# Attention and expert kernel on one core: moving SP's transfers at the change of phase, and one group's row statistics on VectorE

## The chip, the cores and the metric

One Trainium2 chip (trn2), one core. The metric is the device time of one execution in microseconds (us). Of a kernel several executions are timed and the median is given.

## The reference

The input x is (8, 512, 128) in float32: 8 batches of 512 tokens. It is layer-normed, and the result goes two ways: through causal attention with 16 heads of 8 (relu on queries, keys and values, a mask for keys and queries whose row sums to zero, a residual and a layer norm), and through a second norm, a product, eight experts and a last product with gelu. The two are multiplied, with silu on the second, and added to x.

```
xn = layernorm(x)                                # eps 1e-5
Q, K, V = relu(xn @ Wq + bq), relu(xn @ Wk + bk), relu(xn @ Wv + bv)
scores = Q K^T / sqrt(8), causal, masked where a row of xn sums to 0
s = gamma * norm(softmax(scores) V + xn) + beta
f = norm2(xn) @ attn_w.T + attn_b + xn
h = gelu(f_e @ w1[e] + b1[e]);  eo = h @ w2[e] + b2[e]      # expert e takes 256 tokens of each half
g = silu(gelu(eo @ next_w.T + next_b))
out = x + s * g
```

## The kernel before

The program is written engine by engine, with semaphores, in two blocks that meet at a barrier.

**The first phase** (L261 to L793) works batch by batch, i = 0 to 7. VectorE (DVE) norms x: `means` and `variances` per group of tiles (GROUPS, L32: batches 0 to 3, 4 and 5, 6 and 7), then per batch `quotients(i)` (L511) and `sums(i)` (L529), a reduction for the second norm. GpSimd (POOL) refines square roots (`first_roots`, `second_roots`, L346 to L386) and adds up the sums (`totals(i)`, L394). ScalarE (ACT) makes the second norm (`second_norm`, L599, which waits for `totals`) and moves results out of PSUM. TensorE (PE) transposes (`second_normed`, L706, waits for `second_norm`), then projects and runs the experts. Queries and keys go to DRAM as three bf16 parts each: ACT's `split` writes the first (L641, L642), DVE's `rests(i)` (L542) takes the remainder, ACT's `mids` the second, DVE's `lows(i)` (L548) the third. SP stores them (`store_parts`, L251): 4 transfers for queries (one is of constant rows), 5 for keys. On DVE the order in the loop of L569 is quotients(i), sums(i), lows(i-2), rests(i-1). `statistics` (L555) of the last group, `means`, `variances` and `seeds` in one piece, stands at i = 4 behind rests(3), and POOL's `first_roots` of that group waits for its seeds. `hold` (L736) issues products whose result nobody reads; LATE_ROWS (L53) puts 6 before `second_normed(2)` and 8 before `second_normed(5)`.

**The second phase** (L860 on) works in 32 units: batch b, group g of four heads. Keys and queries are stacked on 124 partitions of four tiles: an even batch lies in `q_own`/`k_own`, an odd one in the rooms of the expert weights, `w1_room`/`w2_room` (w_room in the trace). A stack holds the parts (72 rows), a mask row, three rows with the scores' maxima, ones against these (`ones_b`), and 48 fixed rows (`bar_k`, `bar_q`) that carry the causal mask. PE's `chunk` (L1192) makes scores two units ahead for DVE's maxima (L1037, 11 a unit), POOL splits these, PE transposes them (L1210), ACT copies them (`mT`, L1133), and SP writes them as a row into the query stack (L866). PE's unit u starts with a wait for that row (`mrow_in`, L1257), then goes on with the products `keys` (L1213), for ACT's exponentials (L1156), and `values` (L1228).

**SP's queue at the change of phase** is what the change is about. SP waits for the last `lows`, then stores batch 7's parts (9 transfers), issues `load_fixed(sp, 1)` (L174: the fixed rows of the odd stacks, three transfers of 48, 768 and 768 KB), and only then the row for unit 0, `maxima(tok, 0, 0)`. Behind it come per unit the next row and the loads for the unit four further on (7 transfers, `load`). PE meanwhile makes the scores of units 0 and 1 with a product of no use behind each (L1310), to the end of the warm-up.

```
903  sp.wait_ge(low_ready, B)
904  for o in range(2):
905      store_parts(sp, B - 1, o)
906  sp.wait_ge(w2_done, B)
907  load_fixed(sp, 1)
908  maxima(tok, 0, 0)
```

## Time and profile before

| | |
|---|---|
| median of 3 executions | 452.3 us (452.23 to 453.25) |
| the profiled execution | 450.58 us |
| its span in the profile | 448.7 us |
| first phase / second phase, by the trace | 0 to 163.8 us / 163.8 to 448.7 us |
| PE / DVE / ACT / POOL busy | 84% / 82% / 64% / 45% of the span |
| mean granted clock of TensorE | 0.966 of full speed |

Durations and instants in this text are those of the profiled execution; instants count from the start of its span. A row of a timeline gives start, busy time, engine, line, operation, output and inputs, the number of instructions merged into it, and in brackets the idle time before it with what ended it. "SPq" is SP's queue while it issues a transfer; the time on the transfer's way to its place is shown as "DMA" in the chain.

### The profile page before, as it was taken

Reading aid. Unit: us, or ns where it says so; the run is one execution under the profiler, and the core shown is the slowest. Engines: PE = TensorE matmul, PEld = TensorE weight load, DVE = VectorE, ACT = ScalarE, POOL = GpSimd, SP = SyncE. Lnnn points to the kernel's source line nnn. Section 1 sums busy time; section 2 is a strip of 40 time slices with the busy share of each in tenths; the row PEclk is TensorE's granted clock in tenths of the full one; section 3 lists DMA queues with packets and bytes.
Section 4 is the critical chain, followed back from the end, with each engine's and each line's share of the span. In section 5 each row is a group of like instructions: output and inputs, shape, how many; then the busy total and the mean of one; then the engine's idle time right before and its main releaser. Section 6 shows DMA issues by size and latency. Waiting matters only on the chain.

```text
span 448.7 us, 9664 instructions
## 1 busy us (share of the span) xinstructions
PE 375.1 (84%) x3507; PEld 246.3 (55%) x3507; DVE 366.9 (82%) x846; ACT 288.7 (64%) x572; POOL 201.4 (45%) x525
## 2 busy tenths in 40 slices
PE   0046997999799985499999999999999999999950
PEld 0013774787487752366656665566566566656420
DVE  5989998979794257379899898999998998989427
ACT  0004777887588921367877877868778778778740
POOL 8422284417531131002147456556374474565591
PEclk9999999999899999599999999999999999999985
DMA  8920003772545527233332424342422424240000
GB/s 218 329 69 1 1 12 99 172 163 54 154 121 139 139 68 155 37 90 80 89 81 72 121 59 114 82 104 65 125 68 76 119 72 122 59 112 27 3 23 23
DMA packets 32197, 41.71 MB, mean 93 GB/s; under 512 B 5926, under 2 KB 24726, under 8 KB 32150
## 3 DMA queue, kind: packets, MB, share of 16 engines
q1 hardware_dynamic: 31990, 41.08, 34.8%
q8 instruction: 27, 0.44, 0.4%
q14 instruction: 20, 0.16, 0.1%
q0 software_dynamic: 160, 0.03, 0.0%
HBM read 26.43 MB, written 11.02 MB: 83 GB/s over the span
## 4 chain that ended last, share of the span: by engine, by line
PE 43%; DVE 12%; DMA 3%; SPq 2%; issue 2%; ACT 1%; POOL 0%; DVEq 0%; ACTq 0%; POOLq 0%
PE banks L1238 15%; PE banks L1221 8%; PE banks L1201 8%; DVE mx L1037 7%; PE banks L1203 5%; PE banks L1223 5%; DMA q_own<-mT 3%; DVE res L1076 2%; DVE stats L1082 2%; PE banks L1248 1%; SPq L256 1%; ACT pt L1156 1%; SPq L179 1%; PE banks L1210 0%; DVE res L1063 0%
## 5 line engine op out<-in xcount | busy, mean ns | idle before, releaser
L1037 DVE TENSOR_REDUCE mx<-banks 128x1 f32<-128x512 f32 (+3 forms) x352 | 200.9, 635 | 28.3 <-PE banks L1203 26.4
L1156 ACT ACTIVATE pt<-banks 128x512 f32<-128x512 f32 x320 | 169.8, 601 | 56.4 <-PE banks L1223 48.7
L1238 PE MATMUL banks<-pt,vg 128*18 128x512 f32 (+3 forms) x1024 | 81.4, 435 | 0.7 <-ACT pt L1156 0.7
L928 POOL TENSOR_SCALAR mneg<-mx 128x16 f32<-128x16 f32 x32 | 8.1, 253 | 120.7 <-DVE mx L1037 119.5
L1201 PE MATMUL banks<-k_own,q_own 76*128 76x384 bf16 (+2 forms) x192 | 49.9, 283 | 13.2 <-DMA q_own<-mT 10.1
L1201 PE MATMUL banks<-w_room 76*128 76x384 bf16 (+2 forms) x192 | 48.1, 274 | 3.4 <-DVE mx L1037 3.4
L1221 PE MATMUL banks<-q_own,k_own 76*128 76x384 bf16 (+2 forms) x192 | 49.4, 283 | 0.0
L1221 PE MATMUL banks<-w_room 76*128 76x384 bf16 (+2 forms) x192 | 47.5, 275 | 0.9 <-ACT pt L1156 0.5
L1238 PEld LDWEIGHTS banks<-pt,vg 128*18 128x18 f32 x1024 | 23.7, 97 | 43.8 <-issue 33.4
L1203 PE MATMUL banks<-k_own,q_own 124*128 124x128 bf16 x256 | 45.1, 224 | 0.0
L1203 PE MATMUL banks<-w_room 124*128 124x128 bf16 x256 | 43.8, 219 | 0.0
L1223 PE MATMUL banks<-q_own,k_own 124*128 124x128 bf16 x256 | 43.6, 224 | 0.0
L1223 PE MATMUL banks<-w_room 124*128 124x128 bf16 x256 | 42.2, 219 | 0.0
L739 PE MATMUL banks<-bias_rows,ones_p 128*128 128x512 bf16 x44 | 12.3, 437 | 28.1 <-DVEq L502 28.1
L1201 PEld LDWEIGHTS banks<-k_own,q_own 76*128 76x128 bf16 x192 | 19.0, 100 | 24.4 <-DMA q_own<-mT 10.4
L777 PE MATMUL banks<-xaT,w_room 128*128 128x256 f32 x128 | 29.2, 381 | 0.8 <-ACT xaT L620 0.8
L785 PE MATMUL banks<-hid,w_room 128*128 128x256 f32 x128 | 28.9, 379 | 0.0
L677 ACT ACTIVATE hid<-banks,cols_sb 128x256 f32<-128x256 f32 x64 | 26.8, 470 | 1.5 <-PE banks L777 0.9
L1221 PEld LDWEIGHTS banks<-w_room 76*128 76x128 bf16 x192 | 18.7, 97 | 14.8 <-ACT pt L1156 6.3
L1223 PEld LDWEIGHTS banks<-q_own,k_own 124*128 124x128 bf16 x256 | 25.9, 101 | 1.1
L1221 PEld LDWEIGHTS banks<-q_own,k_own 76*128 76x128 bf16 x192 | 19.3, 101 | 13.0 <-issue 4.1
L777 PEld LDWEIGHTS banks<-xaT,w_room 128*128 128x128 f32 x128 | 23.7, 190 | 4.6 <-ACT xaT L620 1.6
(196 smaller groups left out, 732.6 us busy)
## 6 DMA issues: line engine op xcount, KB each, us to landing
k_scratch<-parts SPq DMA_DIRECT2D x40, 128.0 KB, 2.3
k_own<-k_scratch SPq DMA_DIRECT2D x48, 96.0 KB
w_room<-k_scratch SPq DMA_DIRECT2D x48, 96.0 KB
q_scratch<-parts SPq DMA_DIRECT2D x24, 128.0 KB, 2.3
q_own<-q_scratch SPq DMA_DIRECT2D x32, 96.0 KB
w_room<-q_scratch SPq DMA_DIRECT2D x32, 96.0 KB
w_room<-in_w_dram SPq DMA_DIRECT2D x1, 2048.0 KB, 11.9
q_own<-q_scratch SPq DMA_DIRECT2D x16, 112.0 KB
```

The lines of the kernel that those rows point to most:

```text
L677: ins = act.activation(hid[:, h, j, :], banks[:, bank + j // 2, EC * (j % 2):EC * (j % 2) + EC], ACT.Gelu, bias=b1[2 * n + h][j])
L739: mm(banks[:, TRX, :], ones_p[:, :], bias_rows[:, 0:1, :].broadcast_to([P, TB, C]), start=True, stop=True)
L777: ins = mm(banks[:, bank + j // 2, EC * (j % 2):EC * (j % 2) + EC], w1_sb[:, 2 * n + h, P * j:P * j + P], xaT[:, EC * h:EC * h + EC], star ...
L785: ins = mm(banks[:, XB, EC * h:EC * h + EC], w2_sb[:, 2 * n + h, j, :], hid[:, h, j, :], start=(j == 0), stop=(j == HC - 1))
L1037: dve.tensor_reduce(mx[:, u % 2, heads[0]:heads[-1] + 1, q], banks[:, S0 + slots[0] % SLOTS, 0:w * len(heads)].rearrange("p (h k) -> p h k ...
L1076: ins = dve.scalar_tensor_tensor(out=res[:, k, :], in0=att[:, k, :], scalar=live_all[:, at:at + 1], in1=xn_all[:, at, :], op0=ALU.mult, op ...
L1156: act.activation(pt[:, T * j:T * j + T], banks[:, bank(), :], ACT.Exp, scale=SCALE).then_inc(exp_done, 1)
L1201: mm(o[:, 0:w - P], qx[by][0:LIVE, g, h, P * q:P * q + P], kx[by][0:LIVE, g, h, 0:w - P], start=True, stop=True)
L1203: ins = mm(o[:, w - P:w], qx[by][0:STACK, g, h, P * q:P * q + P], kx[by][0:STACK, g, h, w - P:w], start=True, stop=True)
L1221: mm(o[:, P:n], kx[par][0:LIVE, g, h, P * k:P * k + P], qx[par][0:LIVE, g, h, P * k + P:T], start=True, stop=True)
L1223: ins = mm(o[:, 0:P], kx[par][0:STACK, g, h, P * k:P * k + P], qx[par][0:STACK, g, h, P * k:P * k + P], start=True, stop=True)
L1238: ins = mm(banks[32 * h:32 * h + VP, OT, P * k:T], vg[:, g, k, h, :], pt[:, KPLACE[k, h]:KPLACE[k, h] + n], start=(k == 0 and g % 2 == 0), ...
```

## The change

Three edits.

1. The fixed rows are loaded in four pieces, one for each group of heads, each with its own semaphore (three transfers of 12, 192 and 192 KB). For the even stacks the four pieces follow each other where the one load stood. For the odd stacks piece g goes behind the row for unit g + 1, ahead of the loads for the odd batch's group g. PE waits for a piece where it first needs it.
2. Of batch 7's stores the query ones stay ahead of the first row; the five key ones go behind the loads of batch 1's units (two, one, one, one).
3. On DVE the last group's `means` and the centring move to i = 3, its `variances` and `seeds` to i = 4, both ahead of `rests`. The 8 idle products before `second_normed(5)` go.

```diff
-LATE_ROWS = {2: 6, 5: 8}
+LATE_ROWS = {2: 6}
...
-    def load_fixed(sp, par):
-        sp.dma_start(kx[par][MROW + 1:LIVE].rearrange("p g h t -> p (g h) t"),
-                     ones_b[:, :].unsqueeze(1).broadcast_to([PARTS, HEADS, T])).then_inc(fixed_in[par], 16)
+    def load_fixed(sp, par, g):
+        sp.dma_start(kx[par][MROW + 1:LIVE, g],
+                     ones_b[:, :].unsqueeze(1).broadcast_to([PARTS, G, T])).then_inc(fixed_in[par][g], 16)
         for stack, bar in ((kx[par], bar_k), (qx[par], bar_q)):
-            sp.dma_start(stack[LIVE:STACK].rearrange("p g h t -> p (g h) t"),
-                         bar[:, :].unsqueeze(1).broadcast_to([BAR_ROWS, HEADS, T])).then_inc(fixed_in[par], 16)
+            sp.dma_start(stack[LIVE:STACK, g],
+                         bar[:, :].unsqueeze(1).broadcast_to([BAR_ROWS, G, T])).then_inc(fixed_in[par][g], 16)
...
+        def store_keys(sp, i, copies):
+            for k in copies:
+                dst = k_dram[i:i + 1, k].rearrange("b d h t -> (b h) d t")
+                sp.dma_start(dst, parts[:, i % 2, 1, k % PARTS, :]).then_inc(parts_out[i % 2][1], 16)
...
                     if i == 1:
                         sp.wait_ge(bars_ready, 1)
-                        load_fixed(sp, 0)
+                        for g in range(NG):
+                            load_fixed(sp, 0, g)
...
+                    if i == 3:
+                        means(GROUPS[2])
+                        centred(GROUPS[2])
+                    if i == 4:
+                        variances(GROUPS[2])
+                        seeds(GROUPS[2])
                     if i > 0:
                         rests(tok, i - 1)
                     if i == 1:
                         dve.wait_ge(x_in[2], 16)
                         statistics(GROUPS[1])
-                    if i == 4:
-                        statistics(GROUPS[2])
...
                         if not last:
+                            if b == 0:
+                                load_fixed(sp, 1, g)
                             load(b + 1, 1 - par, g)
+                            if b == 1:
+                                store_keys(sp, B - 1, range(g, 2 * PARTS - 1, NG))
...
                 sp.wait_ge(low_ready, B)
-                for o in range(2):
-                    store_parts(sp, B - 1, o)
                 sp.wait_ge(w2_done, B)
-                load_fixed(sp, 1)
+                store_queries(sp, B - 1)
                 maxima(tok, 0, 0)
...
                         if ahead:
-                            if first and g == 2:
-                                pe.wait_ge(fixed_in[1], 48)
+                            if u + 2 < 2 * NG:
+                                pe.wait_ge(fixed_in[(u + 2) // NG][(u + 2) % NG], 48)
```

`store_parts` is split into `store_queries` and `store_keys`, and the first line of `variances`, which subtracts the mean, becomes `centred`; the other calls keep their order.

SP's queue from the barrier on, before. `parts` are batch 7's parts, `mT` the row of maxima, here for units 0 and 1 (two rows in one):

```order
L256 DMA q_scratch<-parts 16x8x512 [waits low_ready]
L256 DMA q_scratch<-parts 16x8x512 x2
L258 DMA q_scratch<-q_fixed 16x4x512
L256 DMA k_scratch<-parts 16x8x512 x5
L176 DMA w_room<-ones_b 3x16x512 [waits w2_done]
L179 DMA w_room<-bar_k 48x16x512
L179 DMA w_room<-bar_q 48x16x512
L866 DMA q_own<-mT 3x16x128 [waits mT_ready] x2
L159 DMA w_room<-q_scratch 24x2048 x2
```

The same place now:

```order
L255 DMA q_scratch<-parts 16x8x512 [waits w2_done,low_ready]
L255 DMA q_scratch<-parts 16x8x512 x2
L256 DMA q_scratch<-q_fixed 16x4x512
L882 DMA q_own<-mT 3x16x128 [waits mT_ready] x2
L176 DMA w_room<-ones_b 3x4x512
L179 DMA w_room<-bar_k 48x4x512
L179 DMA w_room<-bar_q 48x4x512
L159 DMA w_room<-q_scratch 24x2048 x2
```

The five key stores and the fixed rows no longer stand ahead of the first two rows of maxima; a quarter of the fixed rows stands behind the second.

DVE behind sums(4), before: `parts<-rest` is lows(2), `rest<-full` is rests(3), and the statistics of the last group follow, seeds at their end:

```order
L551 TENSOR_TENSOR parts<-rest,parts 128x2x512 [waits mid_ready]
L545 TENSOR_TENSOR rest<-full,parts 128x1024 [waits split_ready,low_ready]
L94 TENSOR_REDUCE s<-x_all 128x128 [waits rest_ready]
L96 TENSOR_TENSOR s<-s 128x64 [waits dve_self]
L97 TENSOR_TENSOR s<-s 128x32 [waits dve_self]
L99 TENSOR_TENSOR s<-s 128x16 [waits dve_self]
L100 TENSOR_TENSOR small<-s 128x8 [waits dve_self]
L451 TENSOR_SCALAR small<-small 128x8 [waits dve_self]
L458 TENSOR_TENSOR xn_all<-x_all,small 128x1024 [waits dve_self]
L459 TENSOR_TENSOR gate_all<-xn_all 128x1024 [waits dve_self]
```

The same place now (rows of the first part stand one batch earlier, between lows(1) and rests(2)):

```order
L560 TENSOR_TENSOR parts<-rest,parts 128x2x512 [waits mid_ready]
L468 TENSOR_TENSOR gate_all<-xn_all 128x1024 [waits low_ready]
L469 TENSOR_REDUCE win<-gate_all 128x32 [waits dve_self]
L471 TENSOR_TENSOR small<-win 128x8 [waits dve_self]
L472 TENSOR_TENSOR small<-small,win 128x8 [waits dve_self]
L473 TENSOR_TENSOR small<-small,win 128x8 [waits dve_self]
L474 TENSOR_SCALAR small<-small 128x8 [waits dve_self]
L475 TENSOR_SCALAR small<-small 128x8 [waits dve_self]
L481 TENSOR_SCALAR small<-small 128x2x8 [waits dve_self]
L482 TENSOR_SCALAR small<-small 128x2x8 [waits dve_self]
L554 TENSOR_TENSOR rest<-full,parts 128x1024 [waits dve_self,split_ready]
L524 TENSOR_TENSOR quo<-xn_all,small 128x512 [waits rest_ready]
```

rests(3) now stands behind the seeds, and quotients(5) right behind rests(3).

## Rows read from the trace of the kernel before

**Rows 1.** Chain of waits in order of time, 163 to 190 us (start us, us, what).
```profile
173.77 11.34 DMA q_own<-mT
```

**Rows 2.** Timeline of SP's queue, the key stores (start us, us, engine line op out<-in).
```profile
166.33 3.93 SPq L256 DMA_DIRECT2D k_scratch<-parts  x5
```

**Rows 3.** Timeline of ACT, second norm of batch 4 and the first row's copy.
```profile
95.71 1.64 ACT L602 ACTIVATE xl_st<-xn_all,shift,small 128x128 f32<-128x128 f32 x4
...
172.50 0.27 ACT L1133 ACTIVATE mT<-banks 48x128 bf16<-48x128 bf16 x1 [10.00 <-PE banks L1210]
```

**Rows 4.** Timeline of PE at the hand-over and at two units' starts.
```profile
174.67 0.38 PE L1310 MATMUL banks<-k_own,q_own 76*128 76x512 bf16 x1
185.16 0.50 PE L1201 MATMUL banks<-k_own,q_own 76*128 76x384 bf16 x1 [10.11 <-DMA q_own<-mT]
...
194.87 0.33 PE L1201 MATMUL banks<-k_own,q_own 76*128 76x384 bf16 x1
...
202.09 0.33 PE L1201 MATMUL banks<-w_room 76*128 76x384 bf16 x1
```

**Rows 5.** Busy time by stretch: us, PE, PEld, DVE, ACT, POOL, granted clock, DMA share, GB/s.
```profile
66.00:71.00 5.00, 2.42 (x12) 1.23 (x10) 4.79 (x13) 1.61 (x5) 3.89 (x10) 1.00 0.62 168
...
116.50:121.00 4.50, 4.50 (x20) 3.43 (x21) 4.31 (x12) 3.40 (x6) 3.46 (x12) 0.64 0.69 202
...
185.00:190.00 5.00, 4.84 (x28) 3.37 (x29) 3.26 (x6) 2.90 (x6) 0.00 (x0) 0.50 0.00 0
```

**Rows 6.** Timeline of PE in the first phase.
```profile
98.23 0.60 PE L709 MATMUL banks<-ident,xl_st 128*128 128x128 f32 x4
...
111.90 1.89 PE L739 MATMUL banks<-bias_rows,ones_p 128*128 128x512 bf16 x8
116.43 0.66 PE L709 MATMUL banks<-ident,xl_st 128*128 128x128 f32 x4 [2.64 <-ACT xl_st L602]
...
131.98 0.66 PE L709 MATMUL banks<-ident,xl_st 128*128 128x128 f32 x4 [0.23 <-ACT xl_st L602]
```

**Rows 7.** Timeline of POOL in the first phase.
```profile
91.55 0.20 POOL L405 TENSOR_TENSOR shift<-shift,small 128x4 f32<-128x4 f32 x1
...
111.96 1.23 POOL L399 TENSOR_TENSOR s<-s 128x32 f32<-128x32 f32 x1
...
114.44 0.20 POOL L405 TENSOR_TENSOR shift<-shift,small 128x4 f32<-128x4 f32 x1
...
125.59 1.10 POOL L399 TENSOR_TENSOR s<-s 128x32 f32<-128x32 f32 x1 [4.72 <-DVE s L532]
126.76 1.15 POOL L400 TENSOR_TENSOR s<-s 128x16 f32<-128x16 f32 x1
```

**Rows 8.** Timeline of DVE in the first phase.
```profile
78.43 1.23 DVE L545 TENSOR_TENSOR rest<-full,parts 128x1024 f32<-128x1024 f32 x1 [1.71 <-ACT parts L642]
...
92.08 1.23 DVE L545 TENSOR_TENSOR rest<-full,parts 128x1024 f32<-128x1024 f32 x1 [1.90 <-ACT parts L642]
...
101.72 0.74 DVE L515 TENSOR_TENSOR quo<-xn_all,small 128x512 f32<-128x512 f32 x1
```

**Rows 9.** Timeline of POOL, the mask's store and its reload.
```profile
153.78 0.77 POOL L424 DMA_DIRECT2D mask_scratch<-maskT  x1 [14.31 <-ACT maskT L670]
156.41 2.03 POOL L171 DMA_DIRECT2D k_own<-mask_scratch  x4 [1.86 <-DMA mask_scratch<-maskT]
```

**Rows 10.** Timeline of DVE, row maxima of two warm-up units and of one unit.
```profile
164.45 12.18 DVE L1037 TENSOR_REDUCE mx<-banks 128x1 f32<-128x512 f32 x22 [4.12 <-PE banks L1203]
...
195.07 6.23 DVE L1037 TENSOR_REDUCE mx<-banks 128x4 f32<-128x512 f32 x11 [1.63 <-PE banks L1203]
```

**Rows 11.** Timeline of the SP queue, one unit's row and loads.
```profile
190.34 1.27 SPq L159 DMA_DIRECT2D w_room<-q_scratch  x3
...
192.88 0.65 SPq L171 DMA_DIRECT2D w_room<-mask_scratch  x1
198.55 0.74 SPq L866 DMA_DIRECT2D q_own<-mT  x1
```

More of the change, by code:

```diff
@@ L150, in build_program @@
     mask_in = sem("first_mask_in")
-    fixed_in = [sem("fixed_in_even"), sem("fixed_in_odd")]
+    fixed_in = [[sem(f"fixed_in{par}_{g}") for g in range(NG)] for par in range(2)]
     banks = ctx.enter_context(nc.psum_tensor("banks", [P, 8, 512], F32))
@@ L249, in build_program, with store_queries @@
         mean, var, a, v2, y, y2, t, t2, s, sh, sl, r, nr, rem, t3 = (small[:, k, :] for k in range(15))
-        def store_parts(sp, i, o):
-            for k in range((PARTS, 2 * PARTS - 1)[o]):
-                part = k_dram[i:i + 1, k] if o == 1 else q_dram[i:i + 1, DH * k:DH * k + DH]
-                dst = part.rearrange("b d h t -> (b h) d t")
-                sp.dma_start(dst, parts[:, i % 2, o, k % PARTS, :]).then_inc(parts_out[i % 2][o], 16)
-            if o == 0:
-                sp.dma_start(q_dram[i, PARTS * DH:QROWS].rearrange("r h t -> h r t"),
-                             q_fixed[:, :, :]).then_inc(parts_out[i % 2][0], 16)
+        def store_queries(sp, i):
+            for k in range(PARTS):
+                dst = q_dram[i:i + 1, DH * k:DH * k + DH].rearrange("b d h t -> (b h) d t")
+                sp.dma_start(dst, parts[:, i % 2, 0, k, :]).then_inc(parts_out[i % 2][0], 16)
+            sp.dma_start(q_dram[i, PARTS * DH:QROWS].rearrange("r h t -> h r t"),
+                         q_fixed[:, :, :]).then_inc(parts_out[i % 2][0], 16)
+        def store_keys(sp, i, copies):
+            for k in copies:
+                dst = k_dram[i:i + 1, k].rearrange("b d h t -> (b h) d t")
+                sp.dma_start(dst, parts[:, i % 2, 1, k % PARTS, :]).then_inc(parts_out[i % 2][1], 16)
         with nc.Block() as block:
@@ L278, in _ @@
                     sp.wait_ge(low_ready, tok.next(low_ready))
-                    for o in range(2):
-                        store_parts(sp, i, o)
+                    store_queries(sp, i)
+                    store_keys(sp, i, range(2 * PARTS - 1))
                     if i == 1:
                         sp.wait_ge(bars_ready, 1)
-                        load_fixed(sp, 0)
+                        for g in range(NG):
+                            load_fixed(sp, 0, g)
                     if 2 <= i < 2 + NG:
@@ L451, in means, with centred @@
                     link(dve.tensor_scalar(mean[:, at], mean[:, at], 1.0 / C, None, ALU.mult))
-                def variances(group):
+                def centred(group):
                     t0, n = group
@@ L458, in variances @@
                     link(tt(cen[:, at, :], xg, mean[:, at].unsqueeze(2).broadcast_to([P, n, C]), ALU.subtract))
+                def variances(group):
+                    at = slice(group[0], group[0] + group[1])
                     link(tt(work[:, at, :], cen[:, at, :], cen[:, at, :], ALU.mult))
@@ L557, in statistics @@
                     means(group)
+                    centred(group)
                     variances(group)
@@ L563, in _ @@
                 means(LOADS[0])
+                centred(LOADS[0])
                 variances(LOADS[0])
@@ L566, in _ @@
                 means(LOADS[1])
+                centred(LOADS[1])
                 variances(LOADS[1])
@@ L903, in _ @@
                 sp.wait_ge(low_ready, B)
-                for o in range(2):
-                    store_parts(sp, B - 1, o)
                 sp.wait_ge(w2_done, B)
-                load_fixed(sp, 1)
+                store_queries(sp, B - 1)
                 maxima(tok, 0, 0)
@@ L1302, in batch @@
                         outputs(tok)
-                pe.wait_ge(fixed_in[0], 48)
                 tok = Tokens(pe)
                 for u in range(2):
+                    pe.wait_ge(fixed_in[0][u], 48)
                     pe.wait_ge(stack_in[0][u], tok.next(stack_in[0][u], UNIT_DMAS))
```

## The prediction

> **What bounds the kernel now.** I read the chain of waits first, in order of time, since the shares of busy time (PE 84%, DVE 82%) tell only that both phases are well filled. Through the second phase the chain lies on PE, unit after unit, and nothing in the change touches a unit from batch 2 on. The place to see is the hand-over between the phases at 163.8 us: the chain runs through SP's queue there, and then, from 173.77 us, 11.34 us through one transfer, the row of maxima for unit 0 [rows 1]. Ahead of that 12 KB row stand five key stores, whose issue alone takes 3.93 us [rows 2], and the fixed rows of the odd stacks, 1.6 MB. The row's data was ready at 172.77 us [rows 3]. PE ends its warm-up at 175.05 us (174.67 + 0.38), then waits 10.11 us for the row and starts unit 0 at 185.16 us [rows 4]. The stretches by clock then show what follows the wait: the granted clock is 0.50 from 185 to 190 us, that is 1.2 GHz, the lower level of the two [rows 5]. Unit 0 takes 9.71 us (194.87 - 185.16), unit 1, mostly at full clock, 7.22 us (202.09 - 194.87) [rows 4].
>
> The second place is in the first phase, which I read by the timelines of PE, DVE and POOL. PE runs without a gap up to 111.90 us, issues the 8 idle products, and then waits 2.64 us, to 116.43 us, for ACT's second norm of batch 5 [rows 6]. ACT waited for POOL's totals(5), at work from 111.96 to 114.64 us [rows 7]. POOL was late because it first had to refine the last group's roots, and their seeds come from the statistics that DVE finished just before quotients(5) at 101.72 us [rows 8]. After it the clock falls too: its mean is 0.64 from 116.5 to 121 us [rows 5].
>
> **The hand-over, step by step.** With key stores and fixed rows gone from in front, SP issues four query stores, is done at about 166.3 us, where the first key store is issued now [rows 2], and waits for the row's data. The row is issued at 172.8 us. Before never shows such a row on an empty queue; the nearest case is the mask's small store, 2.63 us from its issue at 153.78 us to the reload that waits for it at 156.41 us [rows 9]. Bounds: 1.9 us (the idle part of that wait) and 3.9 us (the issue time of the five key stores, as an upper mark for a busy queue). I take 2.6: row there at about 175.5 us, PE idle for 0.4 us. That is 9.7 us sooner than 185.16.
>
> Unit 0 then runs at full clock, since PE's break is 0.4 us instead of 10.1. Three things bound the start of unit 1. PE's own work is at most the 7.22 us of unit 1: 182.7. The second row is issued 3.68 us after a unit's start (198.55 - 194.87) and needs 2.6: 181.8. DVE's 22 warm-up maxima end at 176.63 us and the next 11 take 6.23 us [rows 10]: 182.9, less up to a few maxima that PE may be ahead. I take 182.3, against 194.87: **12.6 us** won at the hand-over, with 11.0 (a slower row and DVE's backlog) and 13.0 as its ends. In other terms 9.7 of these are the wait and 2.9 the clock.
>
> Where the stall goes, the next thing late could be the moved transfers. The fixed rows of a quarter go behind the second row, about 180.0 us. Price of a piece: the whole lot, with the row behind it and what was left of the key stores, took 14.9 us (170.26 to 185.11 [rows 1, 2]), so a quarter is 3.7 us at most if it scales; at the other end only three issues count, at the 0.6 us between a load's 0.46 (3.2 over seven) and a key store's 0.79: 1.9 us. Then come seven loads, issued from 190.34 to 193.53 us before, 3.2 us [rows 11]. So SP is free at 185.1 to 186.9 us, and the row for unit 2 is due at 182.3 + 3.7 = 186.0 and needed at 189.5. Cover is there but thin, about 1 us behind the row's own 2.6. I take 0 and keep 1 us a unit for four units as the far end. PE's six waits for the pieces stand where it waits for the loads issued behind them: 0. The key stores, 5 times 0.8 us of issue [rows 2], fall in batch 1 behind the loads, where SP idles about 5 us a unit (193.53 to 198.55 [rows 11]), and they are read only with batch 7: 0.
>
> **The first phase, step by step.** DVE does the same work in another order. Before, it idles 1.71 us ahead of rests(2) and 1.90 us ahead of rests(3), both times for ACT [rows 8]; now one half of the statistics stands ahead of each. The whole is 8.4 us long (93.31, the end of rests(3), to 101.72), a half about 4, so both gaps are filled: quotients(5) starts 3.6 us sooner, at 98.1 us. quotients(4) starts some 2.5 us later instead. Its totals were ready at 91.75 us [rows 7], and ACT took them up at 95.71 [rows 3]: of the 4.0 us of slack 2.5 go to that, and up to 1.2 to the meeting of totals(4) with DVE's next products. It is thin, but holds: 0, with 0.5 us as the far end. Since rests(3), 1.23 us, now stands behind the seeds instead of ahead, these come 4.9 us sooner, and with them POOL's root refinement and totals(5), at about 107.1 us.
>
> There totals(5) meets lows(3) and rests(4) on DVE. Before, its instructions took 1.23 us and then 0.2 each; totals(6), under the same two DVE operations, took 1.10 and 1.15 for its first two [rows 7]. That is 0.9 us more, so totals(5) ends at 110.7 instead of 114.64, **4.0 us** sooner. The Trainium skill (SBUF, State Buffer, section SBUF: two separate sides) says that DVE with two SBUF inputs and a reading GpSimd operation exclude each other for a whole instruction; by that rule, the trace agrees, it is 4.0, and without it the sum would have 4.9.
>
> PE's second_normed(5) then starts at 112.4 instead of 116.43, and DVE's next batch, which waits for POOL's halves behind the totals, 4.0 us sooner too. From there on all goes the same way: totals(6) is again slow, and second_normed(6) comes at 128.0 instead of 131.98 [rows 6]. PE, at full clock now, would be there at about 126.1 (112.4 and a period of 13.7 us, as from 98.23 to 111.90 [rows 6]), so it idles 1.9 us. The lower clock behind 116.43 therefore gives nothing back, since DVE and POOL, not PE, set 131.98. The idle products gone are 1.89 us of PE that were hidden by the wait; left in, they would end at 113.8 and cost 1.4. The nine more transfers of the even stacks' pieces add some 6 us of issue behind the stores of batch 1; these are 9 issues of 0.7 us in a period of 13.7, and the first loads come a batch later, so 7 us were free: 0.
>
> **Sum.** 12.6 + 4.0 = 16.6 us. Against the profiled execution, 450.58 us, that gives 434.0. The median of the runs shown is 452.3, 1.7 above; the same step gives **435.7 us**.
>
> **Rivals.**
> 1. The clock falls in the first phase, after the new 1.9 us wait at 126 us. Against: between 66 and 71 us PE was busy for 2.42 of 5 us and the clock stayed at 1.00; for: the wait before 116.43 us did bring it down [rows 5]. Price: 15.55 us between 116.43 and 131.98 against 13.7 at full clock, up to 1.9 us: 437.6 us.
> 2. The pieces are slow and delay rows 2 to 5. For: the same transfers held the row for 11.34 us [rows 1]. Against: each is a quarter. At 1 us a unit, four units: 439.7 us. The Trainium skill (DMA: Bandwidth & Descriptors, Bandwidth) speaks against cutting transfers: "Transfers under 64 KB are descriptor-dominated", and its advice is 1 MiB. By that rule the 12 KB pieces and 192 KB pieces cost more than a quarter each, which would lead here; the trace has no piece of this kind.
> 3. The row's wait is not the queue but the row's own way. Then only the issue moves, 173.77 to 172.8, 1 us: 447.3 us. Against: the other 31 rows are never waited for.
> 4. Slower: each piece holds the queue so long that rows 2 to 5 each come late by more than 4.2 us (a quarter of 16.6). That needs a piece of over 8 us, where I have at most 3.7: loads 3.2, piece 8, against a pitch of 7.2. At 14 us a piece, that is, if a piece costs what the whole does, each unit takes 17 us instead of 7.2: 435.7 + 39 = 475 us.
> 5. The change doesn't do what it says: the row is held by the query stores still ahead. Their issue is over at 166.3, 6.5 us ahead of the row's; this goes with rival 3.
>
> **Numbers.** Forecast 0.66, rival 1 0.15, rival 2 0.12, rivals 3 and 5 0.04, rival 4 0.02, and 0.01 for no change at all. A measurement of this kernel can tell about 0.3%, 1.4 us, from no change. Range: low, the hand-over at 13.0, POOL undisturbed (4.9), and a median as low as the profiled run (1.7 less): 432.7, rounded to 432.5. High, rival 2 with 0.8 us to spare: 440.5. Faster 0.97, same 0.01, slower 0.02.
>
> **What would show it.** PE's wait for `mT` under 1 us, the granted clock at 1.0 over the hand-over, unit 0 under 7.5 us; SP's pieces behind the second row, no PE wait for `mT` or the rooms in units 2 to 7; quotients(5) 3.6 us sooner, PE's wait before second_normed(5) under 1 us and before second_normed(6) about 1.9. Wrong would be: new waits for the row in batch 0, a clock under 1 at 128 us, or a barrier that moves by less than 3 us.

## The result and the profile after

The changed kernel takes 434.19 us in the median (433.81 to 434.34, 4 executions) against 452.26 us (451.46 to 453.25, 4): ratio 0.9598, 95% interval 0.9578 to 0.9618. Forecast were 435.7 us, in a range from 432.5 to 440.5. The medians are 18.1 us apart, the two profiled executions only 16.8 us (450.58 and 433.81 us; spans 448.7 and 432.1). In a second comparison, below, the medians were 434.16 and 451.04 us, 16.9 apart; before's own executions spread over more than 2 us, and what goes with that is told at run 10.

The page's first part, and the shares of the chain by engine, after:

```profile
PE 370.1 (86%) x3499; PEld 242.5 (56%) x3499; DVE 365.9 (85%) x846; ACT 288.1 (67%) x572; POOL 204.9 (47%) x525
...
PE 46%; DVE 13%; issue 2%; ACT 1%; POOL 1%; DVEq 0%; ACTq 0%; POOLq 0%
```

SP's queue and the DMA have left the chain; before, the row of maxima alone stood in it for 11.34 us [rows 1]. What the chain through the hand-over shows in their place is DVE at the warm-up's maxima (chain in order of time: start us, us, what):

```profile
160.47 12.19 DVE mx L1055 x22
```

SP's queue at the change of phase, after (start us, us, engine, line, output and input, number of transfers):

```profile
159.92 1.83 SPq L255 DMA_DIRECT2D q_scratch<-parts  x3
161.80 0.59 SPq L256 DMA_DIRECT2D q_scratch<-q_fixed  x1
168.85 6.68 SPq L882 DMA_DIRECT2D q_own<-mT  x2
175.57 0.72 SPq L176 DMA_DIRECT2D w_room<-ones_b  x1
176.33 0.64 SPq L179 DMA_DIRECT2D w_room<-bar_k  x1
177.02 0.61 SPq L179 DMA_DIRECT2D w_room<-bar_q  x1
177.67 2.73 SPq L159 DMA_DIRECT2D w_room<-q_scratch  x3
180.44 1.18 SPq L165 DMA_DIRECT2D w_room<-k_scratch  x3
181.66 0.69 SPq L171 DMA_DIRECT2D w_room<-mask_scratch  x1
182.40 0.77 SPq L882 DMA_DIRECT2D q_own<-mT  x1
```

The row's data is there at 168.78 us (ACT, `mT`), 8.9 us into the second phase, as before (172.77 - 163.84 [rows 3]):

```profile
168.51 0.27 ACT L1151 ACTIVATE mT<-banks 48x128 bf16<-48x128 bf16 x1 [10.00 <-PE banks L1228]
```

PE at the end of the warm-up and at the starts of units 0, 1 and 2:

```profile
170.68 0.38 PE L1328 MATMUL banks<-k_own,q_own 76*128 76x512 bf16 x1
171.13 0.34 PE L1219 MATMUL banks<-k_own,q_own 76*128 76x384 bf16 x1
...
178.46 0.33 PE L1219 MATMUL banks<-k_own,q_own 76*128 76x384 bf16 x1
...
185.68 0.33 PE L1219 MATMUL banks<-w_room 76*128 76x384 bf16 x1
```

PE's warm-up ends at 171.06 us (170.68 + 0.38) and unit 0 starts at 171.13: no wait is left, where 10.11 us stood before [rows 4]. The row was issued at 168.85 us, so its way is at most 2.3 us. Unit 0 takes 7.33 us instead of 9.71, unit 1 again 7.22. Unit 2 starts at 185.68, 16.41 us sooner than before (202.09 [rows 4]). The granted clock, by stretch (us, PE, PEld, DVE, ACT, POOL, then clock, DMA share, GB/s), is full in these stretches. Earlier, from 40 to 50 us, it was below 1.00 in this profile (0.79 and 0.87 in the two halves), where before's has 1.00:

```profile
72.00:76.00 4.00, 4.00 (x18) 2.30 (x17) 3.82 (x10) 3.37 (x6) 0.49 (x1) 1.00 0.03 10
...
128.00:134.00 6.00, 6.00 (x29) 3.93 (x30) 5.68 (x15) 5.34 (x10) 1.13 (x1) 1.00 0.57 161
...
170.00:175.00 5.00, 4.18 (x42) 2.61 (x42) 5.00 (x10) 2.66 (x7) 1.09 (x5) 1.00 0.01 2
175.00:180.00 5.00, 5.00 (x59) 3.08 (x57) 4.43 (x10) 3.82 (x8) 0.45 (x2) 1.00 0.42 91
```

In the first phase, DVE's rests(2) and rests(3) have no idle time ahead of them any more, quotients(5) starts at 98.09 us instead of 101.72, and the next batch at 112.09 instead of 116.07. The first line is from before (its other instants stand in [rows 8]), the rest from after:

```profile
116.07 0.20 DVE L508 RECIPROCAL small<-small 128x8 f32<-128x8 f32 x1 [2.99 <-POOLq L392]
```

```profile
80.92 1.22 DVE L554 TENSOR_TENSOR rest<-full,parts 128x1024 f32<-128x1024 f32 x1
...
96.79 1.27 DVE L554 TENSOR_TENSOR rest<-full,parts 128x1024 f32<-128x1024 f32 x1
98.09 0.69 DVE L524 TENSOR_TENSOR quo<-xn_all,small 128x512 f32<-128x512 f32 x1
...
112.09 0.20 DVE L517 RECIPROCAL small<-small 128x8 f32<-128x8 f32 x1 [2.66 <-POOLq L397]
```

POOL's totals(5), first, second and third operation and the last one:

```profile
107.19 1.09 POOL L404 TENSOR_TENSOR s<-s 128x32 f32<-128x32 f32 x1 [0.60 <-DVE s L541]
108.36 1.15 POOL L405 TENSOR_TENSOR s<-s 128x16 f32<-128x16 f32 x1
109.59 0.20 POOL L407 TENSOR_TENSOR s<-s 128x8 f32<-128x8 f32 x1
...
110.46 0.20 POOL L410 TENSOR_TENSOR shift<-shift,small 128x4 f32<-128x4 f32 x1
```

It starts 4.8 us sooner, but its first two operations take 1.09 and 1.15 us, each to 0.1 us behind the end of the DVE operation beside it (lows(3) ends at 108.17 us, rests(4) at 109.43), and it ends at 110.66 instead of 114.64. PE at second_normed(4), (5) and (6):

```profile
98.08 0.60 PE L725 MATMUL banks<-ident,xl_st 128*128 128x128 f32 x4
...
112.45 0.66 PE L725 MATMUL banks<-ident,xl_st 128*128 128x128 f32 x4 [0.54 <-ACT xl_st L618]
...
127.99 0.66 PE L725 MATMUL banks<-ident,xl_st 128*128 128x128 f32 x4 [1.90 <-ACT xl_st L618]
```

The second phase starts at 159.9 us, 4.0 us sooner (PE's first product of the warm-up at 160.05 instead of 164.03). So the trace shows 4.0 us of gain in the first phase and 12.4 at the hand-over (16.41 - 3.98), forecast as 4.0 and 12.6.

### The profile page after: what moved, and what is told of

It reads as the page before. It is cut to its first block, busy times and chain, and to the rows that moved or that the text cites. A ratio compares the mean times of both kernels' runs of the same rounds, so it can differ in the third digit from the quotient of the medians.

```text
span 432.1 us, 9671 instructions
## 1 busy us (share of the span) xinstructions
PE 370.1 (86%) x3499; PEld 242.5 (56%) x3499; DVE 365.9 (85%) x846; ACT 288.1 (67%) x572; POOL 204.9 (47%) x525
## 4 chain that ended last, share of the span: by engine, by line
PE 46%; DVE 13%; issue 2%; ACT 1%; POOL 1%; DVEq 0%; ACTq 0%; POOLq 0%
PE banks L1256 16%; PE banks L1239 9%; DVE mx L1055 8%; PE banks L1219 8%; PE banks L1221 6%; PE banks L1241 5%; DVE stats L1100 2%; PE banks L1266 2%; DVE res L1094 2%; ACT pt L1174 1%; PE banks L1228 0%; DVE res L1081 0%; DVE res L1084 0%; DVE mixed L1085 0%; DVE aggr L1104 0%
## 5 line engine op out<-in xcount | busy, mean ns | idle before, releaser
L1219 PE MATMUL banks<-k_own,q_own 76*128 76x384 bf16 (+2 forms) x192 | 48.4, 275 | 3.3 <-DVE mx L1055 2.7
L1239 PE MATMUL banks<-q_own,k_own 76*128 76x384 bf16 (+2 forms) x192 | 47.8, 274 | 0.0
L1221 PE MATMUL banks<-k_own,q_own 124*128 124x128 bf16 x256 | 44.0, 219 | 0.0
L1241 PE MATMUL banks<-q_own,k_own 124*128 124x128 bf16 x256 | 42.5, 219 | 0.0
L755 PE MATMUL banks<-bias_rows,ones_p 128*128 128x512 bf16 x36 | 10.6, 456 | 27.9 <-DVEq L511 27.9
L404 POOL TENSOR_TENSOR s<-s 128x32 f32<-128x32 f32 x8 | 8.6, 1070 | 37.9 <-DVE s L541 37.8
L801 PEld LDWEIGHTS banks<-hid,w_room 128*128 128x128 f32 x128 | 24.3, 190 | 3.3
## 6 DMA issues: line engine op xcount, KB each, us to landing
k_scratch<-parts SPq DMA_DIRECT2D x40, 128.0 KB, 2.3
q_scratch<-parts SPq DMA_DIRECT2D x24, 128.0 KB, 2.3
```

What stands on the lines that cost most here:

```text
L755: mm(banks[:, TRX, :], ones_p[:, :], bias_rows[:, 0:1, :].broadcast_to([P, TB, C]), start=True, stop=True)
L801: ins = mm(banks[:, XB, EC * h:EC * h + EC], w2_sb[:, 2 * n + h, j, :], hid[:, h, j, :], start=(j == 0), stop=(j == HC - 1))
L1219: mm(o[:, 0:w - P], qx[by][0:LIVE, g, h, P * q:P * q + P], kx[by][0:LIVE, g, h, 0:w - P], start=True, stop=True)
L1221: ins = mm(o[:, w - P:w], qx[by][0:STACK, g, h, P * q:P * q + P], kx[by][0:STACK, g, h, w - P:w], start=True, stop=True)
L1239: mm(o[:, P:n], kx[par][0:LIVE, g, h, P * k:P * k + P], qx[par][0:LIVE, g, h, P * k + P:T], start=True, stop=True)
L1241: ins = mm(o[:, 0:P], kx[par][0:STACK, g, h, P * k:P * k + P], qx[par][0:STACK, g, h, P * k:P * k + P], start=True, stop=True)
```

## The experiments

Twelve kernels ran, in three sets. The kernels of a set ran on one chip, together with before, whose medians are 451.10 us (runs 1 to 4), 451.04 (5 to 8) and 451.47 (9 to 12). Differences between sets are best read from the ratios to before.

**Run 1, the hand-over alone.** The changed kernel with DVE's old order and the 8 idle products.

```diff
-LATE_ROWS = {2: 6}
+LATE_ROWS = {2: 6, 5: 8}
...
-                    if i == 3:
-                        means(GROUPS[2])
-                        centred(GROUPS[2])
-                    if i == 4:
-                        variances(GROUPS[2])
-                        seeds(GROUPS[2])
...
+                    if i == 4:
+                        statistics(GROUPS[2])
```

> SP's edits alone (fixed rows in pieces, key stores in batch 1); the last group's statistics in one piece at i = 4 and the 8 idle products as before. Theory (the gain is 12.5 us at the hand-over plus 4.0 us in the first phase, and they add up): barrier at 163.8 us as before, PE's wait for the row under 0.5 us, units 0 and 1 at full clock, unit 1 at 178.5 + 4.0 = 182.4 us; ratio to before 0.972, about 439.7 us. Rival (the two parts overlap, since PE's clock at the hand-over also depends on the first phase): under 10 us or over 15 us won.

Measured: 440.21 us (439.26 to 440.35), ratio 0.9745 (0.972 to 0.977), that is 11.5 us. Counted from each barrier, unit 2 starts 25.8 us in (190.77 - 164.95) against 38.3 before (202.09 - 163.84): 12.4 us, as in the whole change. The theory holds, and the rival (under 10 us or over 15 us) is out. The barrier itself lay 1.1 us later in this execution than in before's, since the clock had fallen early in the first phase: it is 0.50 from 45 to 50 us, where before's profile has 1.00.

**Run 2, the statistics alone.** Before's SP and PE, with DVE's new order and LATE_ROWS = {2: 6}.

> The kernel before with DVE's new order for the last group's statistics and without the 8 idle products; SP's queue as before. Theory: barrier 4.0 us sooner (159.8), the wait for the row at the hand-over again about 10 us with half clock behind it; ratio 0.991, about 448.3 us. Rival (the wait at the hand-over depends on when SP's stores of the first phase are through): the wait changes by over 1 us. Beside it, the extra 1.3 us by which the medians differ more than the traces (18.1 against 16.8) should show in this or in the hand-over run.

Measured: 445.83 us (445.24 to 446.36), ratio 0.9874 (0.9849 to 0.9899), 5.7 us; expected were 4. The wait for the row is back, 9.4 us of it. The two ratios multiply to 0.9622, and the whole change, measured again in run 5, has 0.9620: the parts add up and neither hides the other. The 4.0 us lie just outside this part's interval, 4.6 to 6.8 us, and no run shows where the rest comes from. In the profile the barrier is only 3.0 us sooner than before's. The clock fell to 0.58 from 72 to 76 us in this execution, so that PE came to second_normed(5) at 114.03 us without a wait and to second_normed(6) at 128.94, 1.0 us later than in the changed kernel. The way from the barrier to unit 2 takes 37.35 us (198.16 - 160.81) instead of 38.25, since the wait is 0.7 us shorter. SP and PE:

```profile
163.30 3.13 SPq L256 DMA_DIRECT2D k_scratch<-parts  x5
...
181.45 0.50 PE L1212 MATMUL banks<-k_own,q_own 76*128 76x384 bf16 x1 [9.44 <-DMA q_own<-mT]
```

The five key stores were issued in 3.13 us instead of 3.93 [rows 2], and the fixed rows and the row behind them went out 0.8 us sooner. Why one and the same five issues differ by that was not varied.

**Run 3, PE busy while it waits.** It tells how much of the hand-over's gain is clock.

```diff
+                for _ in range(44):
+                    mm(banks[:, ST0 + RING - 1, :], qx[0][0:LIVE, 1, 0, 0:P], kx[0][0:LIVE, 1, 0, :],
+                       start=True, stop=True)
                 for b in range(B):
                     batch(tok, b)
```

> The kernel before with 44 more idle products on PE behind the warm-up (44 x 0.216 = 9.5 us), so that PE is busy while it waits for the row. Nothing else changes. Theory (of the 12.5 us, 9.7 to 10 are the wait and 2.4 to 2.9 the half clock behind it): row lands at 185.1 us as before, the clock stays at 1.0, unit 0 takes 7.3 us instead of 9.7, ratio 0.9945, about 449.8 us. Rival (unit 0 is slow for another reason, traffic or DVE's late start): no gain, ratio 1.000.

Measured: 449.07 us (447.08 to 449.31), ratio 0.9933 (0.9903 to 0.9962), that is 3.0 us where 2.5 were expected; the rival, no gain, is out. PE at units 0 and 1:

```profile
187.17 0.34 PE L1201 MATMUL banks<-k_own,q_own 76*128 76x384 bf16 x1 [1.05 <-DMA q_own<-mT]
...
193.64 0.33 PE L1201 MATMUL banks<-k_own,q_own 76*128 76x384 bf16 x1
```

The row is as late as before (21.75 us behind the barrier at 165.42, before 21.32), and only a wait of 1.05 us is left. Unit 0 now takes 6.47 us instead of 9.71, at 0.34 us a product of 384 columns instead of 0.50. So the half clock behind the wait costs 3.2 us when DVE is idle and ready. The changed kernel gets 2.4 of that back (9.71 - 7.33), since its unit 0 starts with DVE still at the warm-up's maxima.

**Run 4, the fixed rows ahead of the row, the key stores not.**

```diff
+                for g in range(NG):
+                    load_fixed(sp, 1, g)
                 maxima(tok, 0, 0)
...
-                            if b == 0:
-                                load_fixed(sp, 1, g)
```

> The changed kernel, but the odd stacks' fixed rows (all four pieces, 1.6 MB) go ahead of the first row again, behind the query stores; the key stores stay in batch 1. Theory (it is the fixed rows that hold the row, by their transfer time of about 10 us for 1.6 MB from the issue at 162.3 us): row lands at about 174 to 176 us, PE waits 3 to 5 us, the clock may fall behind it: 5 to 8 us above the changed kernel, 439 to 442 us. Rival (key stores and fixed rows matter alike, by their number of transfers): 12 issues of 0.65 us end at 170.1 us, the row would land at 172.4, 1.5 us above, 435.7 us.

Measured: 442.48 us (442.22 to 444.25), ratio 0.9808 (0.9779 to 0.9838), 8.3 us above the changed kernel (434.16 us in run 5), just over the 5 to 8 us expected and far from the rival's 1.5. PE at units 0 and 1:

```profile
178.95 0.50 PE L1219 MATMUL banks<-k_own,q_own 76*128 76x384 bf16 x1 [5.91 <-DMA q_own<-mT]
...
188.81 0.33 PE L1219 MATMUL banks<-k_own,q_own 76*128 76x384 bf16 x1
```

Behind this wait of 5.91 us the clock was 0.50 (180 to 185 us), and unit 0 takes 9.86 us. SP's queue, the first of the twelve transfers and the row:

```profile
164.42 0.80 SPq L176 DMA_DIRECT2D w_room<-ones_b  x1
...
175.24 8.85 SPq L882 DMA_DIRECT2D q_own<-mT  x2
```

The twelve issues take 10.8 us, 0.90 each and not the rival's 0.65, so that the row's issue begins at 175.24 us, when its data has long been ready (170.77), and it lands 3.7 us later, 1.4 more than on the empty queue of the changed kernel. From the first issue of the fixed rows to unit 0 it is 14.5 us here with twelve transfers (178.95 - 164.42) and 14.9 before with three (185.16 - 170.31): the cut by itself made the lot no slower. Before, unit 0 starts 21.3 us behind the barrier, here 17.1. Of these 4.2 us, 3.9 are the issue time of the key stores [rows 2]; the two kernels also differ in the cut of the fixed rows, so this is no clean price.

**Run 5, the changed kernel again,** for comparison with the next three.

> The changed kernel itself, for comparison on the same chip as the next three: ratio to before 0.960, about 434.2 us.

Measured: 434.16 us (433.81 to 434.74), ratio 0.9620 (0.9596 to 0.9644).

**Run 6, the key stores back in front.**

```diff
                 store_queries(sp, B - 1)
+                store_keys(sp, B - 1, range(2 * PARTS - 1))
                 maxima(tok, 0, 0)
...
-                            if b == 1:
-                                store_keys(sp, B - 1, range(g, 2 * PARTS - 1, NG))
```

> The changed kernel with batch 7's five key stores back between the query stores and the first row. Theory (SP has 6.5 us between the query stores' end at 162.4 us and the row's data at 168.8; the stores take 3.9 us of issue and are through by then): the same within 0.3% of the changed kernel, row issued at 168.9. Rival (the stores' traffic holds the row): 1 to 3 us slower.

Measured: 434.33 us (433.92 to 435.94), ratio 0.9632 (0.9608 to 0.9657): no difference from run 5, as the theory had it. The row is issued at 170.92, right behind its data (170.85; the barrier lies later here, since the clock fell at 128 us, see run 10), and unit 0 starts 2.71 us behind the copy (in the changed kernel 2.62). Once the fixed rows are away, moving the key stores is worth nothing; with them in front, it was worth about 4 us (run 4). The two edits of SP's queue are not two gains.

**Run 7, the 8 idle products back** (LATE_ROWS = {2: 6, 5: 8} in the changed kernel).

> The changed kernel with the 8 idle products before second_normed(5) again. What the prediction says: they end at 113.6 us, 1.2 us behind the 112.45 of the changed kernel, and cost 1.2 to 1.4 us. Rival, seen since: second_normed(6) at 128.0 us is set by DVE and POOL, PE idles 1.9 us ahead of it, so the 1.2 us are absorbed there: within 0.3 us of the changed kernel.

Measured: 434.47 us (434.16 to 434.78), ratio 0.9628 (0.9604 to 0.9651): within 0.3 us of run 5. PE:

```profile
112.03 1.89 PE L755 MATMUL banks<-bias_rows,ones_p 128*128 128x512 bf16 x8
113.76 0.60 PE L725 MATMUL banks<-ident,xl_st 128*128 128x128 f32 x4
...
128.30 0.66 PE L725 MATMUL banks<-ident,xl_st 128*128 128x128 f32 x4 [0.94 <-ACT xl_st L618]
```

The products end at 113.76 and second_normed(5) is 1.3 us later than in the changed kernel, but the next one is where DVE and POOL put it: its wait is 0.94 us instead of 1.90. It comes 0.3 us later than in the changed kernel, but so did second_normed(4) ahead of the products (98.37 against 98.08 us).

**Run 8, POOL's halves of the roots ahead of totals(5).**

```diff
-                    totals(tok, i)
-                    if i == 2:
-                        root_halves(GROUPS[1])
                     if i == 5:
                         root_halves(GROUPS[2])
+                    totals(tok, i)
+                    if i == 2:
+                        root_halves(GROUPS[1])
```

> The changed kernel with POOL's root_halves of the last group ahead of totals(5) instead of behind it. POOL idles 0.6 us there. Both theories: DVE's inverses start at 109.5 us instead of 112.1. If a POOL operation waits out DVE's two-input operation (lock): totals(5) now also meets quotients(6), takes 4.4 instead of 3.5 us, second_normed(5) comes 1 us later, but second_normed(6) is then set by PE at 127.2 instead of 128.0: 0.7 us faster than the changed kernel. If not: second_normed(5) stays at 112.5 and second_normed(6) comes at 126.1, 1.9 us faster.

Measured: 435.30 us (434.36 to 435.85), ratio 0.9642 (0.9619 to 0.9664), if anything slower than run 5. POOL, the second and third operation of the halves and the last of totals(5):

```profile
107.11 1.24 POOL L366 TENSOR_TENSOR small<-small 128x8 f32<-128x8 f32 x1
108.43 1.18 POOL L367 TENSOR_TENSOR small<-small 128x8 f32<-128x8 f32 x1
...
112.54 0.28 POOL L410 TENSOR_TENSOR shift<-shift,small 128x4 f32<-128x4 f32 x1
```

Neither number was met, but the mechanism of the first theory was: now the halves take 1.24 and 1.18 us, since they meet lows(3) and rests(4), and totals(5) behind them ends 2.2 us later than in the changed kernel. PE waits 2.58 us ahead of second_normed(5), the clock is at 0.66 from 115 to 120 us, and the next stage lasts 15.1 us, so that second_normed(6) comes at 129.75 us instead of 127.99, with no wait left: PE sets it. That the clock would fall, neither theory had. The small operations only changed places in the queue for the same two DVE operations.

**Run 9, all four pieces together behind the second row.**

```diff
-                            if b == 0:
-                                load_fixed(sp, 1, g)
+                            if b == 0 and g == 0:
+                                for piece in range(NG):
+                                    load_fixed(sp, 1, piece)
```

> The changed kernel with all four pieces of the odd stacks' fixed rows behind the second row of maxima at once, none behind rows 3 to 5. It tells what spreading them is worth. Theory (the queue is FIFO, the lot takes 10 us or more of transfer from 175.6 us, the loads for unit 4 another 3): the row for unit 2 is issued at about 187 us instead of 182.4 and lands at 189 to 191, needed at 185.7: 3.5 to 5.5 us above the changed kernel, 438 to 440 us, with a clock that may fall. Rival (transfers overlap, SP's issue alone counts, 12 times 0.65 us): row for unit 2 at 186.9 + 2.3: 3.5 us at most, and no wait for the loads.

Measured: 444.92 us (444.35 to 445.95), ratio 0.9850 (0.9822 to 0.9878), over 10 us above the changed kernel, two to three times the 3.5 to 5.5 us expected. SP's queue (the first and the last of the 12 issues, the first loads, the row for unit 2), then PE at unit 2:

```profile
176.05 0.72 SPq L176 DMA_DIRECT2D w_room<-ones_b  x1
...
185.98 0.83 SPq L179 DMA_DIRECT2D w_room<-bar_q  x1
186.85 2.91 SPq L159 DMA_DIRECT2D w_room<-q_scratch  x3
...
191.76 0.76 SPq L882 DMA_DIRECT2D q_own<-mT  x1
```

```profile
194.05 0.50 PE L1220 MATMUL banks<-w_room 76*128 76x384 bf16 x1 [7.73 <-DMA q_own<-mT]
```

The 12 issues take 10.8 us instead of the expected 7.8, the seven loads behind them 4.9 instead of 3.2, and the row for unit 2 goes out at 191.76 us. PE waits 7.73 us, unit 2 takes 10.4 us at half clock. So the rival was right that SP's issues hold the row, which lands 2.3 us behind its own issue, but each issue took longer than it had. It is the first mistake of before again, one row later. Spreading the pieces is a large part of the gain: all at once behind the second row, they give back 10 of the 12.4 us. Whether three large transfers in that place would do the same was not run.

**Run 10, 8 idle products ahead of second_normed(6)** (LATE_ROWS = {2: 6, 6: 8}).

> The changed kernel with 8 idle products before second_normed(6), where PE idles 1.9 us. Theory (that wait brings the clock down in some executions and not in others, at 1.5 us when it does: 15.15 against 13.5 us to the next second_normed): the waits there shrink to 0.2 us, the clock stays at 1.00 from 128 to 134 us, fastest executions as the changed kernel's, slowest ones 1 us faster; median 0 to 1 us below the changed kernel. Rival (idle products cost as such): 0.3 us or more above it.

Measured: 434.29 us (433.89 to 435.09), ratio 0.9614 (0.9587 to 0.9641). In its profile the wait is gone and the clock is 1.00 from 128 to 134 us, but the median does not move. In this profiled execution the clock had fallen earlier, at 72 us, so PE came late to second_normed(6) anyway. The run leaves open what the products are worth in the mean.

That a wait of the same length brings the clock down in one execution and not in another is seen in profiles whose first phase is the same program. Run 5 and run 9 from 72 to 76 us, both behind a wait of 2.65 to 2.67 us ahead of second_normed(2) (columns as above):

```profile
72.00:76.00 4.00, 4.00 (x17) 3.07 (x15) 3.64 (x11) 2.62 (x5) 0.06 (x1) 0.57 0.11 33
```

```profile
72.00:76.00 4.00, 4.00 (x21) 2.53 (x20) 3.79 (x12) 3.51 (x6) 0.04 (x1) 1.00 0.12 33
```

And run 6 from 128 to 134 us, behind the wait of 1.90 us ahead of second_normed(6); the same stretch of the changed kernel, shown in the section on the result, has 1.00 behind the same wait:

```profile
128.00:134.00 6.00, 5.61 (x22) 4.01 (x23) 5.75 (x16) 3.87 (x7) 0.72 (x1) 0.72 0.63 171
```

In run 5 the stage behind second_normed(2) lasts 15.14 us, in run 9 13.49. In run 6 the stage behind second_normed(6) lasts 15.15 us, in the changed kernel 13.49. Each fall costs 1.7 us at its place; of the one in run 5, 0.9 us are left at second_normed(6) (128.87 us against 127.99), since later waits take up the rest. Over all fourteen profiles a wait ahead of second_normed(2) came out at 2.6 to 2.7 us in seven, and the clock fell behind five of them; behind the wait of 1.9 us ahead of second_normed(6) it fell in two of four; behind waits of 2.58 to 2.64 us ahead of second_normed(5) in all four. The wait ahead of second_normed(2) is itself not fixed: in the other profiles it is 1.0 to 1.3 us or none, and in each of those, and in none of the seven, the clock had been below 1.00 from 45 to 50 us, so that PE came later. What decides a fall was not varied.

The times of before's 28 executions of the three sets go along with this: the eight with a mean clock of 0.969 or 0.970 took 449.97 to 450.58 us, the five with 0.957 or 0.958 took 451.25 to 454.22 us.

**Run 11, a version meant to beat both.** The totals of batches 5 and 6 are added up on DVE, and the last group's halves follow its roots on POOL.

```diff
+ON_DVE = (5, 6)
...
+                def totals_here(i):
+                    at = slice(TB * i, TB * i + TB)
+                    dve.wait_ge(lanes_ready, i + 1)
+                    dve.wait_ge(sums_ready, i)
+                    dve.wait_ge(seconds_ready, 2 if i < 6 else 3)
...
                     sums(i)
+                    if i in ON_DVE:
+                        totals_here(i)
...
-                    if i == 5:
-                        root_halves(GROUPS[2])
...
                     if i == 4:
                         first_roots(tok, GROUPS[2])
+                        root_halves(GROUPS[2])
```

> A version meant to beat both: the changed kernel with the totals of batches 5 and 6 (six small operations) on DVE instead of POOL, right behind sums, and the last group's root_halves right behind its first_roots on POOL. DVE gets 2 x 1.25 us of work, and no POOL operation waits for DVE's two-input operations on the path. Theory (second_normed(5) and (6) were set by POOL's totals, held by DVE): second_normed(5) at 111.75 and (6) at 125.4 instead of 128.0, both without a wait, barrier 2.6 us sooner, 431.6 us. Rival (DVE is the bound itself): the 1.25 us come on top, second_normed(6) at 127 or later, 0 to 1 us won.

Measured: 433.16 us (431.56 to 433.36), ratio 0.9576 (0.9545 to 0.9607). No wait is left at second_normed(5) and (6), but the clock had fallen at 72 us in this execution, and they come at 113.53 and 127.19 us, PE alone setting them. The expected 431.6 us were not met in the median, and the 1.0 us won and the 127.19 us would fit the rival as well, but its cause doesn't: PE waited for nobody, it came late itself. Two of the six executions took 431.56 and 431.97 us, at a mean clock of 0.986 and 0.983, the other four 433.14 to 433.36 at 0.973 to 0.979: the forecast fits the executions with the higher clock.

**Run 12, the same with 12 idle products ahead of second_normed(2)** (LATE_ROWS = {2: 12}).

> As the run before, with 12 instead of 6 idle products before second_normed(2), which shortens PE's wait there from up to 2.7 us to about 1.3. Theory (the clock falls there in some executions, 0.57 from 72 to 76 us in one profile and 1.00 in others, at 1.5 us each time): as the run before or up to 0.7 us faster in the median, no fall at 72 us in the profile. Rival: no change.

Measured: 431.75 us (431.00 to 432.48), ratio 0.9555 (0.9528 to 0.9583). PE at second_normed(5) and (6), 13.67 us apart:

```profile
112.37 0.60 PE L748 MATMUL banks<-ident,xl_st 128*128 128x128 f32 x4
...
126.04 0.60 PE L748 MATMUL banks<-ident,xl_st 128*128 128x128 f32 x4
```

The barrier lies at 158.1 us, 1.8 us ahead of the changed kernel's, and the profiled span is 430.5 us. It is the fastest of all runs, 2.4 us under the changed kernel's 434.16 in the medians (all of its six executions lie below all of the changed kernel's eight), though the intervals of the two ratios, 0.9528 to 0.9583 and 0.9596 to 0.9644, come from two sets. Between runs 11 and 12 alone the intervals overlap. As expected, the clock is 1.00 from 72 to 76 us in its profile, but it had been 0.77 from 45 to 50 us, so that PE came late to second_normed(2) anyway: what the added products are worth is not shown.

## Why the prediction was right

**The wait for the row.** Right: it was the queue in front of the row, and above all the fixed rows (run 4, which has them there without the key stores). The row's way, taken as 2.6 us from the mask's store, is at most 2.3; unit 0 starts right at the end of the warm-up instead of 0.4 us behind it. Rivals 3 and 5 are out.

**The clock behind it.** Right in kind and size: 9.7 us of wait and 2.9 of clock were forecast; run 3 shows the clock by itself, 3.2 us in unit 0, and the changed kernel has 2.4 (9.71 - 7.33). Of the three bounds for unit 1, 182.3 us was chosen, 6.8 us for unit 0; it took 7.33, so the upper two, DVE's backlog and PE's own 7.22, were the nearer. Counted from the barrier, the wait gave back 10.05 us instead of 9.7 and the clock 2.38 instead of 2.9. That the hand-over falls only 0.2 us short of 12.6 is in part luck: two errors of opposite sign.

**The moved transfers.** That they would be hidden, with about 1 us to spare, was right, and rival 2 is out for the changed kernel: no wait for a row appears in its profile. The price was put together wrongly. Three issues take 2.06 us, at the low end of 1.9 to 3.7, but the seven loads behind them take 4.7 us (177.67 to 182.35) instead of 3.2, and the next row is issued at 182.40, 0.3 us behind its data. The transfers slow the issues behind them, and that the terms left out. Run 9 shows it at full size, with a row that comes 7.73 us late. It doesn't bear out rival 4: there the four pieces together took 10.8 us of issue, 2.7 each, and none cost what the whole does. The bound of 3.7 us for a quarter agrees with run 4, where the whole lot took 14.5 us.

**The key stores.** The prediction let both edits of SP's queue share one gain and did not ask what each is worth. Run 6: once the fixed rows are away, the key stores' part is 0. The cut of the even stacks' fixed rows was not undone by itself.

**The first phase.** The step was right to 0.1 us at each station: 98.1 (98.09) for quotients(5), 110.7 (110.66) for the end of totals(5), 112.4 (112.45) and 128.0 (127.99) for the second norms, 1.9 us of wait ahead of the last. That DVE's two-input operations hold POOL's decided between 4.0 and 4.9; the first two operations of totals(5) end with lows(3) and rests(4), and run 8 moved the same holds onto other operations. The Trainium skill (SBUF, State Buffer, section SBUF: two separate sides) calls this an exclusive lock for the whole instruction, and the trace agrees: 1.09 and 1.15 us in place of the 0.2 us that such operations take alone.

**What failed.** The step "left in, they would end at 113.8 and cost 1.4", on the idle products. They end there, and cost nothing (run 7), because second_normed(6) waits for DVE and POOL. The prediction said so itself two sentences earlier and did not apply it. So LATE_ROWS is no part of the gain. The sum isn't touched, since the products were priced at 0 where they are gone.

**The median.** The profiled execution was forecast at 434.0 us and took 433.81. The median was forecast at 435.7 us and came out 1.5 below, since before's median then, 452.3 us, lay 1.7 above its profiled execution, while the changed kernel's four executions lie within 0.53 us. From before's median in run 5's set, 451.04 us, the same step gives 434.4 us, and 434.16 were measured. So the 1.5 us lay in the median that the step was taken from.

**Rival 1** was priced rightly (up to 1.9 us, 1.7 seen) and misjudged in kind. It is no property of the change: the fall comes in some executions and not in others, with before's first phase (run 3 at 72 us, not in before's profile) as well as with the changed one, after waits of 1.9 to 2.7 us.

**Rival 2's rule.** The Trainium skill (DMA: Bandwidth & Descriptors, section Bandwidth) advises large transfers; its figures there are for loads from HBM. The prediction took from it that pieces cost more than a quarter each. The trace doesn't show that: the lot took 14.9 us with three transfers and 14.5 with twelve (run 4). The 10 us between run 9 and the changed kernel are no matter of size, both have the same twelve; what counts there is who stands behind them in the queue.

## What to carry to other kernels

Look in a queue for what stands ahead of the small transfer that an engine waits for, and put large ones behind it in pieces that fit between two such transfers; all together they only move the wait to the next (run 9). A gap on TensorE can cost more than its length: about 10 us of waiting here took 2.4 to 3.2 us more through the clock. When several things are moved away at once, undo each by itself, since only one of them may have been worth it.

## What the runs showed of the hardware

A wait of 1.9 to 2.7 us on TensorE brought the granted clock down in some executions of the same first phase and not in others (0.57 in run 5 against 1.00 in run 9, from 72 to 76 us), at 1.7 us a time; waits of 5.91, 7.73, 9.44 and 10.11 us brought it down in every profile that has one. SP's issues take longer under traffic: 12 transfers of fixed rows in a row were issued at 0.90 us each (runs 4 and 9) where three alone take 0.69, and the loads behind three of them at 0.67 us each instead of 0.46. GpSimd operations of 0.2 us took 1.09 to 1.24 us beside a DVE operation with two SBUF inputs of 128x1024, and moving them handed the hold to others (run 8).
